# Small model on one core: half of the second MLP product as three float32r matmuls instead of one float32 product

## What is computed

```python
h = jnp.einsum('blv,dv->bld', x, Win) + bin
def body(h, p):
    y = jax.nn.silu(layernorm(h, l1w, l1b))
    y = sconv(y, pr + 1j * pi, lr + 1j * li)       # a complex decay along the sequence
    h = h + y * scl
    y = layernorm(h, l2w, l2b)
    y = jax.nn.silu(jnp.einsum('bld,fd->blf', y, w1) + b1_)    # 128 -> 512
    y = jnp.einsum('blf,df->bld', y, w2) + b2_                 # 512 -> 128
    return (h + y, None)
h, _ = jax.lax.scan(body, h, xs)                   # four layers
return jnp.einsum('bld,vd->blv', layernorm(h, lnl_w, lnl_b), Wout) + bout
```

## Time and profile before

| | |
|---|---|
| Median of 3 runs (lowest to highest) | 1832.55 us (1831.14 to 1834.01) |
| Profiled execution, its own time | 1833.98 us |
| Its span in the profile | 1832.3 us |
| PE busy, share of the span | 1723.3 us, 94% |
| DVE | 1066.5 us, 58% |
| ACT | 654.6 us, 36% |
| POOL | 436.3 us, 24% |
| Share of the chain that ended last | PE 82%, DVE 4%, DMA 4%, ACT 3%, POOL 2% |
| of that, the second MLP product (PE ps L825) | 7% |
| Granted clock of TensorE, mean | 0.96 of 2.4 GHz |

### The profile page before, as it was taken

The page is one execution under the profiler, slowest core; times in us unless marked ns, Lnnn a source line. Parts: engine busy times, 40 slices in busy tenths (PEclk is TensorE's granted clock), DMA queues, the critical chain, the costliest instruction groups (busy, mean ns, idle before and its releaser), DMA issues.

```text
span 1832.3 us, 23328 instructions
## 1 busy us (share of the span) xinstructions
PE 1723.3 (94%) x8154; PEld 1382.9 (75%) x8154; DVE 1066.5 (58%) x2049; ACT 654.6 (36%) x967; POOL 436.3 (24%) x380
## 2 busy tenths in 40 slices
PE   5999999999999999998699999997599899899898
PEld 4788888888888888887566666665478678678686
DVE  5433443345555555575577777766467567567553
ACT  2433333333333333222244545544233333333321
POOL 3111111100000000000366777743112112112110
PEclk9999999999999999999789999997699999899999
DMA  6323333333333332322010000004436536536421
GB/s 242 104 92 116 112 118 118 118 125 111 111 103 117 107 111 102 142 75 90 26 44 35 1 1 1 1 25 162 169 118 227 174 119 225 182 111 219 147 101 58
DMA packets 81543, 199.78 MB, mean 109 GB/s; under 512 B 9747, under 2 KB 26131, under 8 KB 81171
## 3 DMA queue, kind: packets, MB, share of 16 engines
q1 hardware_dynamic: 60690, 129.07, 21.5%
q10 hardware_dynamic: 20736, 69.22, 9.4%
HBM read 125.89 MB, written 72.35 MB: 108 GB/s over the span
## 4 chain that ended last, share of the span: by engine, by line
PE 82%; issue 4%; DVE 4%; DMA 4%; ACT 3%; POOL 2%; SPq 1%; ACTq 0%; POOLq 0%; DVEq 0%
PE ps L643 18%; PE ps L645 17%; PE ps L644 17%; PE ps L825 7%; PE ps L657 3%; PE ps L770 3%; PE ps L816 2%; PE ps L817 2%; PE ps L815 2%; DMA a_in<-in_expert_a 2%; PE ps L776 2%; PE ps L731 1%; PE ps L793 1%; PE ps L707 1%; PE ps L709 1%
## 5 line engine op out<-in xcount | busy, mean ns | idle before, releaser
L643 PE MATMUL ps<-wall_x,x_hi 128*128 128x512 f32 x1008 | 401.6, 398 | 10.7 <-DVE wall_x L1276 5.3
L645 PE MATMUL ps<-wall_x,x_lo 128*128 128x512 f32 x1008 | 396.1, 393 | 0.0
L644 PE MATMUL ps<-wall_x,x_hi 128*128 128x512 f32 x1008 | 395.7, 393 | 0.0
L1838 POOL TENSOR_TENSOR rstd<-var_eps,minus_half 128x1 f32<-128x1 f32 x96 | 77.2, 804 | 933.6 <-DVE minus_mean L1311 926.6
L1302 DVE BATCH_NORM_STATS2 stats<-row 128x6 f32<-128x512 f32 x192 | 133.0, 694 | 182.0 <-ACT row L996 177.6
L643 PEld LDWEIGHTS ps<-wall_x,x_hi 128*128 128x128 f32 x1008 | 191.5, 190 | 55.4 <-issue 13.3
L645 PEld LDWEIGHTS ps<-wall_x,x_lo 128*128 128x128 f32 x1008 | 191.2, 190 | 41.2
L644 PEld LDWEIGHTS ps<-wall_x,x_hi 128*128 128x128 f32 x1008 | 191.7, 190 | 38.4
L643 PE MATMUL ps<-wall_y,x_hi 128*128 128x512 f32 x512 | 204.0, 398 | 2.8 <-POOL wall_y L1845 2.8
L645 PE MATMUL ps<-wall_y,x_lo 128*128 128x512 f32 x512 | 200.4, 391 | 0.0
L644 PE MATMUL ps<-wall_y,x_hi 128*128 128x512 f32 x512 | 200.3, 391 | 0.0
(11 more groups left out here) (236 smaller groups left out, 2944.4 us busy)
## 6 DMA issues: line engine op xcount, KB each, us to landing
x_scratch<-row ACTq DMA_DIRECT2D x64, 512.0 KB, 2.8
x_in<-x_scratch SPq DMA_DIRECT2D x64, 512.0 KB, 4.0
w_in<-in_w_t SPq DMA_DIRECT2D x96, 256.0 KB, 3.0
cx<-x_scratch SPq DMA_DIRECT2D x32, 512.0 KB, 4.2
x_scratch<-cx ACTq DMA_DIRECT2D x32, 512.0 KB, 2.7
out<-row ACTq DMA_DIRECT2D x32, 512.0 KB, 2.6
x_in<-in_x_t SPq DMA_DIRECT2D x29, 512.0 KB, 3.4
w_more<-in_w_t SPq DMA_DIRECT2D x32, 256.0 KB, 3.6
```

The costliest lines, as they stand in the source:

```text
L643: pe.matmul(bank, hi[:, k], wall[:, k, 0, cols], start=(k == 0), stop=False)
L644: pe.matmul(bank, hi[:, k], wall[:, k, 1, cols], start=False, stop=False)
L645: return pe.matmul(bank, lo[:, k], wall[:, k, 0, cols], start=False, stop=(k == KC - 1))
L1838: pool.tensor_tensor(rstd[:, i:i + 1], var_eps[:, i:i + 1], minus_half[:, 0:1], ALU.pow)\
```

## The change

For each layer, the last two of the four 128-row chunks of the second MLP product (`back(2)`, `back(3)`) go over to three float32r matmuls each; the first two stay as they are. For that:

- after `centre_w2` in turn 4, ACT makes `w2_hi` and DVE makes `w2_lo` of the two last chunks of all four layers, 128 x 1024 each
- in each turn ACT writes `g_hi` behind the silu of `hidden(2)` and of `hidden(3)` (Identity, 128 x 512, each behind a wait for the silu)
- in each turn DVE writes `g_lo` twice (128 x 512), between `take_var1` and `scan(1)`
- some semaphores are merged: `bias1_loaded` and `bias3_loaded`; `wout_loaded` and `bout_loaded`; `stats_ready`, `c_stats_ready` and `w_diag` go over to DVE's own counter

The new tiles lie in the first 16 KB of `wall_x`, which is written again when the last dense block's weights come; ACT waits for the last second product before it does so.

```diff
+    w2_hi = at("w2_hi", X, [P, LAYERS, 2, P], F32R)
+    w2_lo = at("w2_lo", X + 4096, [P, LAYERS, 2, P], F32R)
+    g_hi = at("g_hi", X + 8192, [P, 2, HALF], F32R)
+    g_lo = at("g_lo", X + 12288, [P, 2, HALF], F32R)
...
@@ tensor, back(i)
-                    pe.matmul(ps[:, OUT], w2[:, FCH * (n // UNITS) + i], g[:, i], start=(i == 0),
-                              stop=(i == FCH - 1)).then_inc(o_done, 1)
+                    l = n // UNITS
+                    if i < 2:
+                        pe.matmul(ps[:, OUT], w2[:, FCH * l + i], g[:, i], start=(i == 0), stop=False)\
+                          .then_inc(o_done, 1)
+                        return
+                    pe.wait_ge(g_lo_ready, 2 * n + i - 1)
+                    if n == 0:
+                        pe.wait_ge(w2_lo_ready, 1)
+                    pe.matmul(ps[:, OUT], w2_hi[:, l, i - 2], g_hi[:, i - 2], start=False, stop=False)
+                    pe.matmul(ps[:, OUT], w2_hi[:, l, i - 2], g_lo[:, i - 2], start=False, stop=False)
+                    pe.matmul(ps[:, OUT], w2_lo[:, l, i - 2], g_hi[:, i - 2], start=False, stop=(i == FCH - 1))\
+                      .then_inc(o_done, 1)
...
@@ scalar, weight_hi / silu_hidden / turn 4
+                if n == BATCHES * PARTS:
+                    act.wait_ge(o_done, FCH * MLP_END)
...
+                    if i >= 2:
+                        act.wait_ge(g_ready, FCH * n + i + 1)
+                        act.activation(g_hi[:, i - 2], g[:, i], ACT.Identity).then_inc(g_hi_ready, 1)
...
+                    act.wait_ge(w2_ready, 1)
+                    act.activation(w2_hi[:], w2_parts(w2[:]), ACT.Identity).then_inc(w2_hi_ready, 1)
...
@@ vector
-                dve.bn_stats(stats[:, i, half], row[:, i, cols]).then_inc(stats_ready, 1)
+                mark(dve.bn_stats(stats[:, i, half], row[:, i, cols]))
...
-                after(dve.tensor_tensor(w2[:], w2[:], mean, ALU.subtract))
+                dve.tensor_tensor(w2[:], w2[:], mean, ALU.subtract).then_inc(w2_ready, 1)
+                dve.wait_ge(w2_hi_ready, 1)
+                dve.tensor_tensor(w2_lo[:], w2_parts(w2[:]), w2_hi[:].bitcast(F32), ALU.subtract).then_inc(w2_lo_ready, 1)
+
+            def g_low(i):
+                def step(n):
+                    dve.wait_ge(g_hi_ready, 2 * n + i - 1)
+                    dve.tensor_tensor(g_lo[:, i - 2], g[:, i], g_hi[:, i - 2].bitcast(F32), ALU.subtract)\
+                       .then_inc(g_lo_ready, 1)
+                return step
...
-                     ("a", take_var1), ("c", scan(1)), ("b", rotate)]
+                     ("a", take_var1), ("g", g_low(2)), ("g", g_low(3)), ("c", scan(1)), ("b", rotate)]
```

More of the change, by code:

```diff
@@ L89, in part_place @@
     return n // PARTS, k, o, o == k * P // HALF
-def diagonals(n):
-    return sum(part_place(i)[3] for i in range(n + 1))
 def w_slot(n):
@@ L330, in build @@
         evac_act, evac_dve = sem("evac_act"), sem("evac_dve")
-        stats_ready, ve_ready = sem("stats_ready"), sem("ve_ready")
+        ve_ready = sem("ve_ready")
         rstd_ready, shift_ready, normed = sem("rstd_ready"), sem("shift_ready"), sem("normed")
         stored = [sem(f"stored{i}") for i in range(2)]
-        bias1_loaded, bias3_loaded = sem("bias1_loaded"), sem("bias3_loaded")
+        bias_loaded = sem("bias_loaded")
         a_loaded = [sem(f"a_loaded{i}") for i in range(2)]
@@ L339, in build @@
         a_hi_ready, a_lo_ready = sem("a_hi_ready"), sem("a_lo_ready")
-        w_diag, w_product, w_summed = sem("w_diag"), sem("w_product"), sem("w_summed")
+        w_product, w_summed = sem("w_product"), sem("w_summed")
         w_hi_ready, w_lo_ready, w_lo_pool = sem("w_hi_ready"), sem("w_lo_ready"), sem("w_lo_pool")
@@ L349, in build @@
         table_done = sem("table_done")
-        wout_loaded, bout_loaded, row_product = sem("wout_loaded"), sem("bout_loaded"), sem("row_product")
+        readout_loaded, row_product = sem("readout_loaded"), sem("row_product")
         bias_rows_ready, brow_ready = sem("bias_rows_ready"), sem("brow_ready")
@@ L570, in _ @@
             sp.wait_ge(evac_dve, 2 * TILES)
-            sp.dma_start(wout[:], a["wout_t"]).then_inc(wout_loaded, 16)
-            sp.dma_start(bias_rows[:], a["bout"].partition_broadcast(P)).then_inc(bout_loaded, 16)
-            sp.dma_start(bias3[:], a["bias3"].partition_broadcast(P)).then_inc(bias3_loaded, 16)
+            sp.dma_start(wout[:], a["wout_t"]).then_inc(readout_loaded, 16)
+            sp.dma_start(bias_rows[:], a["bout"].partition_broadcast(P)).then_inc(readout_loaded, 16)
+            sp.dma_start(bias3[:], a["bias3"].partition_broadcast(P)).then_inc(bias_loaded, 16)
             sp.wait_ge(brow_ready, 2)
@@ L760, in readout_bias @@
             def readout_bias():
-                pe.wait_ge(wout_loaded, 16)
+                pe.wait_ge(readout_loaded, 2 * 16)
                 pe.wait_ge(evac_dve, 2 * TILES)
@@ L1293, in half_stats @@
                     if s == A_END:
-                        dve.wait_ge(bias1_loaded, 16)
+                        dve.wait_ge(bias_loaded, 16)
                     if s == B_END:
-                        dve.wait_ge(bias3_loaded, 16)
+                        dve.wait_ge(bias_loaded, 2 * 16)
                     dve.wait_ge(mm_done, mm_count(s, half))
@@ L1333, in weight_sum @@
                     diag = part[:, first:first + P]
-                    dve.tensor_tensor(diag, diag, ident[:], ALU.add).then_inc(w_diag, 1)
-                    dve.wait_ge(w_diag, diagonals(n))
+                    after(dve.tensor_tensor(diag, diag, ident[:], ALU.add))
                 dve.wait_ge(w_product, n + 1)
@@ L1575, in bias_sum @@
                 dve.wait_ge(row_product, 1)
-                dve.wait_ge(bout_loaded, 16)
+                dve.wait_ge(readout_loaded, 2 * 16)
                 for half in range(2):
@@ L1613, in residual @@
                     dve.wait_ge(c_added, 2 * c + half + 1)
[L1614 to L1615 removed]
+                    mark(dve.bn_stats(c_stats[:, i, half], place[:, cols]))
+                settle()
                 after(dve.bn_aggr(c_mean_var[:, i], c_stats[:, i].rearrange("p a b -> p (a b)")))
```

13 lines of the change are left out of this document (8 added, 5 removed).

## The result

The changed kernel takes 1858.35 us, the median of four runs (1850.97 to 1862.21), against 1831.85 for the kernel before (four runs, 1824.74 to 1834.01). The ratio on record is 1.0132 with a 95% interval from 1.0096 to 1.0168: slower by 18 to 31 us. (The quotient of the two medians is 1.0145, inside that interval.) The profiled execution took 1856.26, 22.3 more than that of the kernel before. The prediction was 1853, with a range from 1836 to 1859.

What follows compares the result with a forecast made beforehand. TensorE bounded the kernel, and the change would make the VectorE-GpSimd-TensorE loop the bound. 22 turns +17.6 to +21.6, start +2.3, covered turns -2.2 to -2.9 us, added to 1832.55, gave 1853, range 1836 to 1859.

Steps and rivals of the forecast that it cites:

- The ring: Middle turns: two VectorE subtractions lengthen the loop variance, root2, spread, `scale2` by 1.22 us against 1.07 slack; turn 10.72, +0.98.
- The port: Shared SBUF access: x_rot and first scan become ready together, GpSimd wins over VectorE, the scan ends at 4.56; chance 0.52.
- the first rival: Middle turns: VectorE's scan wins SBUF access over x_rot; +0.29 us a turn, 6.4 in 22, total 1839; chance 0.22.
- The rule on the lock: Shared SBUF access: root1 would hold the second g_lo; turn 11.5, 22 turns +39 us, 1872; chance 0.06, low clock included.
- The clock: TensorE in middle turns: some run at 1.2 GHz after idling, costing 1.7 us of work; 0.8 more a turn, 17.6 in 22.
- The start: Start of the stage, turns 4 to 5: splitting w2 on ACT and DVE delays the next `scale2` without cover, +2.3 us.
- The turns with cover: Turns 7 to 9 and 33 to 36: TensorE's saving of 0.31 to 0.42 us each counts, 2.2 to 2.9 back.
- ACT has room: ScalarE in a turn: two splits of 0.63 us fit, 5.1 + 1.3 of 9.7 us; only the second g_lo waits.
- The sum of 17 to 22: Whole kernel: 22 turns +17.6 to +21.6 us, start +2.3, covered turns -2.2 to -2.9; 1850 to 1855, taken as 1853.

Runs made afterwards that it cites:

- e1: Changed kernel with whole float32 matmuls for all four chunks again, splits and subtractions kept: median 1859.18 us, ratio 1.0146 to the kernel before.
- e2: Changed kernel with the new matmuls only, on a constant tile, no splits of g, two chunks left out of the result: 1822.02 us, ratio 0.9933.
- e11: Changed kernel with g_lo(3) behind the variance, hidden(1) ahead of the last two chunks on TensorE, w1 and w2 splits later: 1840.29 us, ratio 1.004.
- e5: Changed kernel without any high and low parts, only the merged semaphores and added ScalarE wait left: 1830.83 us, ratio 0.9989 to the kernel before.
- e3: Changed kernel with only the last chunk in high and low parts, chunks 0 to 2 whole: 1839.42 us, ratio 1.0028 to the kernel before.
- e6: Changed kernel with only the last chunk in parts and GpSimd's rotation of x waiting for the first scan: 1837.08 us, ratio 1.0022.
- e9: Changed kernel with one chunk in parts, its low part behind the variance but ahead of any residual, w1 and w2 splits later: 1836.16 us, ratio 1.002.
- e10: Changed kernel with one chunk in parts and the w1 split moved behind silu(3) and the variance: 1840.73 us, ratio 1.0034.
- e12: Changed kernel with one chunk in parts, VectorE's rotation of x moved behind the variance, w1 and w2 splits later: 1829.66 us, ratio 0.9998.
- e4: Changed kernel with one wait added, GpSimd's rotation of x waiting for the same turn's first scan: 1848.9 us, ratio 1.0088 to the kernel before.

## Why the prediction was right, and where it wasn't

**The ring** was right. The earlier trace rows gave a walk that ended at 10.72; the turns are of 10.70, with the variance at 8.72 (8.73 forecast), root2 at 8.95 (8.97), the rotations' end at 1.74 (1.74). e1 and e2 separate its two halves: the splitting steps on VectorE and ScalarE without the new matmuls make the 10.70, the matmuls alone 9.35. No run has ScalarE's splits without VectorE's, but in none of the 22 turns of the changed kernel does VectorE wait for g_hi. The 1.75 from root2 to the next `scale2` held in the changed kernel (1067.42 to 1069.17).

**The port** was right, and it was the thinnest step. Scan and rotation tie in 20 of 22 turns, and GpSimd wins each. With a lead of 0.44 the scan wins, and the turn is the 10.06 of the first rival. That GpSimd would win a tie I had from one row; the runs bear it out, but it was little to rest 0.52 on.

**The rule on the lock** (the Trainium skill, "SBUF — State Buffer", section "SBUF: two separate sides") would have had root1 hold the second g_lo. Root1 runs from 1063.76 to 1065.14, right beside it, and the two g_lo take 1.28, the scan behind them 1.27. The row I went by, L1517 beside root1, told the truth; the measurement decides. The other way round the rule does hold here: root1 itself is held by the g_lo that is under way when it starts (the last section).

**The clock** was wrong as a step for the 22 turns, and it hardly showed. I took some turns to run at 1.2 GHz behind a gap of about 1 us, from one row with a gap of 1.06. In the changed kernel TensorE stands idle for about 0.9 us in each of 22 turns, where I had counted 1.3, and the granted clock is 1.00 in all of them. A gap of that size doesn't decide by itself: in turn 35 a gap of 1.09 was followed by 0.66, and one of 1.10 at the same place in e11 by 1.00. My low end of 17.6 for the 22 turns came from that step; without it the walk gives 21.6, and 20.99 was measured.

**The start** was 2.26 for 2.3.

**The turns with cover** were sized wrongly. I had 2.2 to 2.9 us back for seven turns (7 to 9 and 33 to 36); together they gave 0.39. Turn 7 gave 0.39, turns 33, 34 and 36 gave 0.36, 0.36 and 0.38, as TensorE's saving should. But turn 8 gave nothing; turn 9 gave 1.47, where the kernel before had run at a granted clock of 0.66 and the changed one had not; and turn 35 lost 2.53. Turn 6, which I had put at nothing within 0.5, gave 1.31, and most of that is the clock too: TensorE is busy throughout that turn in both kernels, at a mean granted clock of 0.85 over 11.38 us before and of 0.94 over 10.07 after, and e1, with the old matmuls, has 10.35 at 0.94. The low stretch had fallen more into turn 5 (0.69 and not 0.81), which is 8.95 long either way.

For turn 35 the step that failed is "ACT has room": I looked at who waits for ScalarE's split in a middle turn, and not at what is queued behind it in a readout turn, the normalisation of a tile and behind that `square2`. ScalarE, TensorE, and the granted clock of the changed kernel there:

```profile
1256.69 1.24 ACT L1145 ACTIVATE cx<-cx,c_shift,c_rstd 128x1024 f32<-128x1024 f32 x1
...
1258.39 0.63 ACT L1109 ACTIVATE squares<-h 128x512 f32<-128x512 f32 x1 [0.46 <-ACT cx L1145]
```

```profile
1259.07 1.05 PE L777 MATMUL ps<-mean_col,squares 128*128 128x1 f32 x8 [1.09 <-ACT squares L1109]
```

```profile
1260.00:1265.00 5.00, 5.00 (x17) 3.97 (x17) 1.11 (x5) 1.21 (x2) 1.53 (x2) 0.66 0.68 206
```

That turn takes 11.62 in the kernels with the old matmuls and no split of g (before, e5) and 12.08 to 12.13 with one split (e3, e6, e9, e10, e12): the cost grows with what stands ahead of the square on ScalarE. With two splits it takes 14.15 to 14.53 in the changed kernel, e1 and e4, but 12.56 in e11, where TensorE waits just as long for the square (1.10). What differs is the granted clock: 1.00 over that turn in e11 and 0.88 in the other three. So of the 2.53 lost about 1.6 go with the low clock behind the gap (14.15 against 12.56) and 0.9 with the wait. e11 has another order on TensorE too, so the shares aren't exact.

**The total.** The sum of 17 to 22 met the stage, 21.4, and about met the profiled execution, 22.3, at its upper end. The 22 turns and the start carry it, and they are as forecast; but that the rest came out near is in part luck, since the 1.31 of turn 6 and the 1.47 of turn 9, both mostly the clock's, stand in for what turn 35 lost. The median of 1858.35 is 5 above my 1853. One part is the value I took inside the sum; the rest is within what one kernel's runs differ by (11 us for the changed kernel's four).

## What to carry to other kernels

Before adding a step to an engine that looks half idle, walk the closed loops that it stands in, and compare the step with the smallest slack of a loop, not with the engine's idle time: VectorE had 1.66 us idle and the ring 1.07. Then try the step in other places of the same list: the same instructions on VectorE cost 10.70, 10.43 or, with one change on TensorE, 9.77 a turn here, and moving an old step that nobody waits for (the rotation) bought the room that no place of the new one did. And ask whether a late step makes itself late again in the next turn; such a loop has two speeds, one small push decides, and a walk of a single turn doesn't show it.
